# Attention operands of a half loaded in two transfers from relaid scratch, shared weights loaded later, and a new order of the first task's units

## The chip, the cores and the metric

The kernel runs on one core of one Trainium2 chip. Its time is device microseconds of one execution, and the result is compared by the median of several runs. TensorE is PE in the profile, VectorE is DVE, ScalarE is ACT, GpSimd is POOL and SyncE is SP. SP computes nothing here. It issues transfers, and its queue in the profile is SPq.

## The reference, cut to what matters

One transformer layer with modulated layer norms: causal attention with low-rank projections, then a router that sends each token to two of eight experts, and a shared feed-forward branch. Two batches of 1,024 tokens, 128 channels, 16 heads of 8 dimensions.

```python
h = _layernorm(x) * (1 + ca) + sa
Q = ((h @ W_dq) @ W_uq).reshape(B, S, 16, 8)
K = ((h @ W_dkv) @ W_uk).reshape(B, S, 16, 8)
V = ((h @ W_dkv) @ W_uv).reshape(B, S, 16, 8)
attn = softmax(where(causal, Q @ K.T / sqrt(8), -inf))
x = x + ga * (attn @ V) @ W_o
h = _layernorm(x) * (1 + cb) + sb
x = x + gb * (shared_ffn(h) + sum over the 2 chosen experts of w * expert_ffn(h))
```

## The kernel before, in words

**Operands in three parts.** A float32 score is built on PE from bf16 operands. Each of Q and K is split into three bf16 parts, hi, mid and lo. A head has 8 dimensions, so all nine products of parts make a contraction over 3 x 3 x 8 = 72 rows. Lines 840 (hi), 1066 (residue on DVE), 849 (mid) and 613 (lo on POOL) make the parts in the tile `parts`; `QK` numbers the eight pieces (batch, key or query, half of 512 tokens), and the first four (numbers 0 to 3: key and query of half 0, key and query of half 1, batch 0) are made up front, before the unit loop. SP writes the parts to scratch in DRAM (`k_parts`, `q_parts`) and reads them back into the tile `S3`, where each part stands three times, in the pattern that crosses every part of Q with every part of K.

**Tasks.** A task is a batch and a group of four heads, so there are eight, 0 to 7. A task has two halves c of 512 queries. `S3` has three buffers. `load(t)` (three transfers of K by `load_k`, line 477, and three of Q for each half by `load_q`, line 485) waits until the scratch of its batch is written (`parts_out`) and, from task 3 on, until the buffer's last user is done. Task 0 has its own quick path: `store_first` (line 456) and loads of each half alone, counted by `first_in0` and `first_in1`. `store_parts` (lines 463 and 469) writes what the other tasks need.

**Two passes over the scores.** The first pass finds each query's maximum: a `max` unit is up to four matmuls (line 1612) into one of three banks, and a reduction on DVE (line 1231 with the causal mask, line 1235 without). A task has 38 max units, 0 to 10 for half 0 and 11 to 37 for half 1. `maxima` negates them, POOL splits them in three parts (lines 654 to 657), PE turns them (`turn`, line 1621), DVE copies them (line 1252), and SP writes them as three more rows of Q (`neg_rows`, line 502, `negT`). The second pass is 38 `score` units a task (line 1643, with the mask at line 1648), each followed by an exponential on ACT (line 894) and by `weigh`, the products with V (line 1665).

**The order.** `attention_order` writes one list for all engines by hand: 20 max units (`AHEAD`), then for each score unit one score and one max unit, but three max units for each of the first ten scores (`CATCH_UP`). `BETWEEN` puts other work behind named max units: the late turns of x (`xturn`, line 1531), the projections of batch 1 (`proj`, line 1536) and the values (`val`, line 1548). These and the max units share the ring of three banks, save `xturn`. PE takes the list in order, so that a unit that waits holds up all behind it. The matmuls of `fill` (line 1818) compute nothing: two behind each of the first 20 max units, one behind each of the first ten scores.

**SP's order.** SP issues the loads of x and of the small weights, then nine transfers of late weights (line 512: router, `be2`, `bs2`, biases, shared expert; DVE first needs them in `gates_out`, in task 2's max units), then `store_first` and the loads of half 0, the same for half 1, `store_parts(0)`, `neg_rows(0, 0)`, `load(1)`, `neg_rows(0, 1)`, `load(2)`, and from then on `neg_rows` and one load a task.

**After attention** come 39 tiles of routed experts, the gather and the output. The change doesn't touch them.

Of the kernel before, what the change touches and what calls it, by code (L numbers as in the profile page):

```python
# [13 lines left out]
ALU = mybir.AluOpType  # L14
# [3 lines left out]
BF16 = mybir.dt.bfloat16  # L18
# [32 lines left out]
def score_units():  # L51

    out = []
    for c in range(2):
        for j in range(4 * c + 4):
# [19 lines left out]
CATCH_UP = 10  # L75
# [4 lines left out]
BETWEEN = {(0, 7): [("xturn", 2, 0)], (0, 10): [("xturn", 3, 0), ("proj", 4, 0), ("proj", 5, 0)],  # L80
           (0, 14): [("proj", 6, 0)], (0, 18): [("proj", 7, 0)], (0, 23): [("val", 2, 0)], (0, 28): [("val", 3, 0)],
# [26 lines left out]
def attention_order(tasks):  # L108
# [26 lines left out]
    for g in range(tasks * NU):  # L135
# [3 lines left out]
        for _ in range(3 if g < CATCH_UP else 1):  # L139
            next_max()  # L140
# [68 lines left out]
def adaln_layer(nc, x, cT, wmod, wdqT, wdkvT, wuq, wuk, wuv, wo, wr1, br1, wr2, br2,  # L209
# [27 lines left out]
    NLOAD = 9  # L237
# [10 lines left out]
    with ExitStack() as ctx:  # L248
# [3 lines left out]
        def sem(name):  # L252
# [128 lines left out]
        kd = nc.dram_tensor("k_parts", [B, NQ, DK, 3, HQ, S], BF16, kind="Internal").ap()  # L381
        qd = nc.dram_tensor("q_parts", [B, 2, 3, NQ, DK, HQ, HALF], BF16, kind="Internal").ap()
# [11 lines left out]
            var_ready std_ready xn_ready xT_ready hT_ready qk_ready hi_ready r1_ready mid_ready lo_ready  # L394
# [33 lines left out]


        @block.sync  # L430
        def _(sp):
# [17 lines left out]
            def store_first(half):  # L449

                cols = slice(HALF * half, HALF * half + HALF)
                for kq in range(2):
                    for part in range(3):
                        sp.wait_ge((s["hi_ready"], s["mid_ready"], s["lo_ready"])[part], done(0, kq, half))
                        dst = qd[0, half, part, 0] if kq else kd[0, 0, :, part, :, cols]
                        sp.dma_start(dst,
                                     parts[0:HQ * DK, kq, part, cols]).then_inc(s[("k_out", "q_out")[kq]], 16)

            def store_parts(b):
                u0 = 0 if b else 1  # L460
                for part in range(3):
                    sp.wait_ge((s["hi_ready"], s["mid_ready"], s["lo_ready"])[part], done(b, 0, 1))
                    sp.dma_start(kd[b, u0:NQ, :, part, :, :].rearrange("u d h n -> (u d) h n"),
                                 parts[DK * HQ * u0:P, 0, part, b * S:(b + 1) * S]).then_inc(parts_out[b], 16)
                for part in range(3):
                    sp.wait_ge((s["hi_ready"], s["mid_ready"], s["lo_ready"])[part], done(b, 1, 1))
                    for c in range(2):
                        cols = slice(b * S + HALF * c, b * S + HALF * c + HALF)
                        sp.dma_start(qd[b, c, part, u0:NQ, :, :, :].rearrange("u d h n -> (u d h) n"),
# [1440 lines left out]
```

## Time and profile before

| what | value |
|---|---|
| three runs | 446.93, 447.58, 448.43 us; median 447.58 us |
| profiled execution | span 445.2 us from the first to the last instruction, mean granted clock 0.969; its own time is not listed apart from the three runs |
| PE busy | 397.4 us, 89% of the span |
| DVE busy | 326.0 us, 73% |
| ACT busy | 265.9 us, 60% |
| POOL busy | 142.9 us, 32% |
| share of the chain that ended last | PE 69%, DVE 14%, issue 5%, DMA 5% |

The span is 2.4 us below the median of the runs, which also hold what lies before the first and behind the last instruction. Busy shares are averages over stages: the first 25 us set up task 0, 25 to 290 us is attention, 290 to 424 us the experts, and the rest the gather and the output.

### The profile page before, as it was taken

Reading aid. Unit: us, or ns where it says so; the run is one execution under the profiler, and the core shown is the slowest. Engines: PE = TensorE matmul, PEld = TensorE weight load, DVE = VectorE, ACT = ScalarE, POOL = GpSimd, SP = SyncE. Lnnn points to the kernel's source line nnn. Section 1 sums busy time; section 2 is a strip of 40 time slices with the busy share of each in tenths; the row PEclk is TensorE's granted clock in tenths of the full one; section 3 lists DMA queues with packets and bytes.
Section 4 is the critical chain, followed back from the end, with each engine's and each line's share of the span. In section 5 each row is a group of like instructions: output and inputs, shape, how many; then the busy total and the mean of one; then the engine's idle time right before and its main releaser. Section 6 shows DMA issues by size and latency. Waiting matters only on the chain.

```text
span 445.2 us, 9323 instructions
## 1 busy us (share of the span) xinstructions
PE 397.4 (89%) x2901; PEld 231.8 (52%) x2901; DVE 326.0 (73%) x1187; ACT 265.9 (60%) x609; POOL 142.9 (32%) x237
## 2 busy tenths in 40 slices
PE   6679889989999999999989899999989999999900
PEld 3335433443443543545533443434767889999900
DVE  5747799888888887889796887735687665555527
ACT  3623647647666766667665566787756755555632
POOL 2520350000010020105576333504177575334410
PEclk9959999999999999999999999999999999999975
DMA  5433321044040120210210000493012233210153
GB/s 151 144 112 109 94 58 54 1 104 148 1 110 1 35 77 0 67 45 0 68 45 18 21 21 18 116 315 70 7 54 67 73 91 95 68 36 27 37 194 102
DMA packets 28819, 31.77 MB, mean 71 GB/s; under 512 B 4851, under 2 KB 23387, under 8 KB 28267
## 3 DMA queue, kind: packets, MB, share of 16 engines
q1 hardware_dynamic: 26067, 26.12, 21.1%
q0 software_dynamic: 2272, 4.67, 3.1%
q8 instruction: 23, 0.38, 0.4%
q10 hardware_dynamic: 432, 0.39, 0.3%
q14 instruction: 25, 0.20, 0.2%
HBM read 21.04 MB, written 9.85 MB: 69 GB/s over the span
## 4 chain that ended last, share of the span: by engine, by line
PE 69%; DVE 14%; issue 5%; DMA 5%; ACT 3%; POOL 2%; SPq 1%; DVEq 0%; ACTq 0%; POOLq 0%
PE oacc L1665 14%; PE mx L1612 12%; PE sc L1643 11%; PE sc L1798 6%; PE oacc L1811 6%; DVE mxp L1235 3%; DVE masked L1231 3%; PE sc L1648 2%; PE sc L1818 2%; PE mx L1765 2%; PE mx L1674 2%; ACT osb L903 2%; POOL slot_rows L734 2%; PE mx L1754 1%; DMA parts<-token_results 1%
## 5 line engine op out<-in xcount | busy, mean ns | idle before, releaser
L894 ACT ACTIVATE pr<-sc 128x512 f32<-128x512 f32 (+1 forms) x296 | 154.0, 579 | 87.3 <-PE sc L1648 47.6
L1612 PE MATMUL mx<-S 72*128 72x512 bf16 (+3 forms) x384 | 112.8, 331 | 13.6 <-DMA S<-q_parts 6.1
L1231 DVE CUSTOM_DVE_ANT_0 masked<-mx,later 128x128 f32<-128x128 f32 (+3 forms) x256 | 111.6, 485 | 17.0 <-PE mx L1612 16.1
L1643 PE MATMUL sc<-S 75*128 75x512 bf16 (+3 forms) x373 | 108.1, 328 | 0.0
L1235 DVE TENSOR_REDUCE mxp<-mx 128x1 f32<-128x512 f32 x128 | 82.5, 684 | 20.9 <-PE mx L1612 20.5
L1665 PE MATMUL oacc<-pr,vb 128*32 128x512 f32 (+3 forms) x768 | 73.9, 493 | 0.0
L1612 PEld LDWEIGHTS mx<-S 72*128 72x128 bf16 x384 | 34.7, 99 | 52.2 <-DVE mxp L1231 14.8
L958 ACT ACTIVATE pr<-sc,bcur 128x128 f32<-128x128 f32 x156 | 44.6, 369 | 26.6 <-PE sc L1798 26.5
L1643 PEld LDWEIGHTS sc<-S 75*128 75x128 bf16 x373 | 34.5, 97 | 46.4 <-issue 21.2
L740 POOL DMA_INDIRECT token_results<-S,xrow x39 | 39.1, 1003 | 48.0 <-DVE S L1372 44.6
L654 POOL CAST neg<-negm 128x16 bf16<-128x16 f32 x16 | 3.2, 198 | 139.7 <-DVE negm L1244 139.7
L1798 PE MATMUL sc<-xTg,vb 128*128 128x128 f32 x312 | 41.6, 276 | 2.6 <-ACT xTg L950 2.5
L1811 PEld LDWEIGHTS oacc<-vb,pr 128*128 128x128 f32 x312 | 39.0, 192 | 7.2 <-issue 6.0
L1648 PE MATMUL sc<-after,identb 128*128 128x128 bf16 (+2 forms) x172 | 41.9, 244 | 0.0
L1811 PE MATMUL oacc<-vb,pr 128*128 128x128 f32 x312 | 41.3, 275 | 0.3 <-ACT pr L958 0.3
L734 POOL DMA_INDIRECT slot_rows<-parts,rowi x32 | 31.6, 986 | 30.2 <-PE sc L1648 13.6
L1798 PEld LDWEIGHTS sc<-xTg,vb 128*128 128x128 f32 x312 | 37.9, 192 | 3.6 <-ACT xTg L950 3.3
L1665 PEld LDWEIGHTS oacc<-pr,vb 128*32 128x32 f32 x768 | 19.0, 108 | 31.1 <-issue 15.9
L1357 DVE COPY vb<-S 128x512 f32 x39 | 18.4, 472 | 20.8 <-issue 11.3
L1372 DVE TENSOR_TENSOR S<-oacc,be_sb 128x128 f32<-128x128 f32 x39 | 11.3, 290 | 18.0 <-PE oacc L1811 16.4
L1231 DVE DVE_READ_ACCUMULATOR2_ANT mxp<- 128x1 f32 x256 | 21.0, 82 | 0.0
L1648 PEld LDWEIGHTS sc<-after,identb 128*128 128x128 bf16 x172 | 16.8, 98 | 7.4
(279 smaller groups left out, 471.2 us busy)
## 6 DMA issues: line engine op xcount, KB each, us to landing
S<-q_parts SPq DMA_DIRECT2D x48, 96.0 KB
S<-k_parts SPq DMA_DIRECT2D x21, 192.0 KB
xrow<-slot_rows SPq DMA_DIRECT2D x39, 64.5 KB, 1.8
S<-in_we SPq DMA_DIRECT2D x1, 2048.0 KB, 9.1
S<-in_we SPq DMA_DIRECT2D x4, 512.0 KB, 9.9
parts<-token_results SPq DMA_DIRECT2D x4, 512.0 KB, 5.7
x_sb<-in_x SPq DMA_DIRECT2D x4, 256.0 KB, 4.0
out_y<-attn SPq DMA_DIRECT2D x4, 256.0 KB, 2.3
```

What stands on the lines that cost most here:

```text
L734: pool.indirect_dma_start(xd, bass.IndirectOffsetOnAxis(ap=rowi[:, g, k, n:n + 1], axis=0), rowsk[:, g % 2, n, k, :], None).then_inc(sent[ ...
L740: pool.indirect_dma_start(yd, bass.IndirectOffsetOnAxis(ap=xrow[:, i % XR, C:C + 1].bitcast(I32), axis=0), yst[:, i % ROWS, :], None).then ...
L894: act.activation(pr[:, group % NBUF, h:h + n, at:at + w], src, ACT.Exp, scale=float(DK) ** -0.5).then_inc(s["exp_done"], 1)
L958: ins = act.activation(hid[:, i % 2, P * f:P * f + P], sc[:, i % 2, P * f:P * f + P], ACT.Silu, bias=bcur[:, i % FREE, f:f + 1])
L1231: ins = dve.tensor_tensor_reduce(masked[:, d % 2, w * m:w * m + w], unit[a][:, w * m:w * m + w], later[:, HALF - w:HALF], 1.0, LOWEST, ALU ...
L1235: ins = dve.tensor_reduce(mxp[:, c, place, h:h + n, i - 4 * c], unit[a][:, 0:n * w].rearrange("p (h n) -> p h n", h=n), AX_X, ALU.max)
L1612: ins = pe.matmul(dst[:, w * m:w * m + w], S3[0:CROSS, r3, 1, q:q + P], S3[0:CROSS, r3, 0, kk:kk + w], start=(m == 0), stop=True, skip_gro ...
L1643: ins = pe.matmul(dst[:, w * m:w * m + w], S3[0:CROSS + 3, r3, 0, kk:kk + P], S3[0:CROSS + 3, r3, 1, q:q + w], start=(m == 0), stop=True, ...
L1648: ins = pe.matmul(dst[:, 0:n * w].rearrange("p (h n) -> p h n", h=n)[:, :, 0:P], identb[:, :], after[:, 0:n, :], start=False, stop=True, s ...
L1665: ins = pe.matmul(oacc[VW * h:VW * h + VW, c, at:HALF], vb[:, t % 2, j, h, :], pr[:, group % NBUF, h, at:HALF], start=(j == 0), stop=(j == ...
L1798: ins = pe.matmul(sc[:, i % 2, P * f:P * f + P], wcur[:, i % 2, P * f:P * f + P], xTg[:, i % 2, :], start=True, stop=True)
L1811: ins = pe.matmul(oacc[:, i % 2, 0:P], hid[:, i % 2, P * f:P * f + P], wcur[:, i % 2, FF + C * f:FF + C * f + C], start=(f == 0), stop=(f ...
```

## The change

Scratch is laid out anew: `k_parts` by half and part, `q_parts` by half with the parts innermost beside the dimension. The operand rows of a half then load in one transfer for K (72 rows from a source of 24 x 3, each row repeated three times in place) and one for Q (72 rows from a source of 3 x 24, the whole block of 24 rows repeated). A task's load is 4 transfers for 9. The stores are 6 for K and 6 for Q for 3 and 6, and the store of K has an outer extent of three head groups in batch 0 and four in batch 1. The late weights go behind `load(2)`. `store_first` alternates K and Q. `store_parts` becomes `store_keys`, ahead of `neg_rows(0, 0)`, and `store_queries`, behind it. The lo part of piece 1 moves from POOL to DVE, between three and five of the eight statistics of x; ACT takes `hi(2)` ahead of `root(2)`; `residue(3)` goes behind the root's refinement. Fillers are 12 for 50. The first 14 scores are followed by 2 x 9, 4 x 2 and 2 x 3 max units for 3 x 10 and 1 x 4, so that the first max unit of task 1 comes behind score 9 for score 6, and from score 14 on the max units are 38 ahead of the scores for 40.

```diff
-CATCH_UP = 10
+MAXES_AFTER = [2] * 9 + [4] * 2 + [2] * 3
+FILLERS = {(0, k): 2 if k < 3 else 1 for k in (0, 1, 2, 3, 4, 5, 7, 8, 10)}
-BETWEEN = {(0, 7): [("xturn", 2, 0)], (0, 10): [("xturn", 3, 0), ("proj", 4, 0), ("proj", 5, 0)],
-           (0, 14): [("proj", 6, 0)], (0, 18): [("proj", 7, 0)], (0, 23): [("val", 2, 0)], (0, 28): [("val", 3, 0)],
+BETWEEN = {(0, 6): [("xturn", 2, 0)], (0, 9): [("xturn", 3, 0)], (0, 11): [("proj", 4, 0)], (0, 14): [("proj", 5, 0)],
+           (0, 17): [("proj", 6, 0)], (0, 21): [("proj", 7, 0)], (0, 26): [("val", 2, 0)], (0, 31): [("val", 3, 0)],
...
-        for _ in range(3 if g < CATCH_UP else 1):
+        for _ in range(MAXES_AFTER[g] if g < len(MAXES_AFTER) else 1):
...
-        kd = nc.dram_tensor("k_parts", [B, NQ, DK, 3, HQ, S], BF16, kind="Internal").ap()
-        qd = nc.dram_tensor("q_parts", [B, 2, 3, NQ, DK, HQ, HALF], BF16, kind="Internal").ap()
+        kd = nc.dram_tensor("k_parts", [B, 2, NQ, 3, DK, HQ, HALF], BF16, kind="Internal").ap()
+        qd = nc.dram_tensor("q_parts", [B, 2, NQ, DK, 3, HQ, HALF], BF16, kind="Internal").ap()
...
-                for kq in range(2):
-                    for part in range(3):
-                        sp.wait_ge((s["hi_ready"], s["mid_ready"], s["lo_ready"])[part], done(0, kq, half))
-                        dst = qd[0, half, part, 0] if kq else kd[0, 0, :, part, :, cols]
+                for part in range(3):
+                    for kq in range(2):
+                        sp.wait_ge(*part_done(part, QK.index((0, kq, half))))
+                        dst = qd[0, half, 0, :, part] if kq else kd[0, half, 0, part]
...
+            def store_keys(b):
+                u0 = 0 if b else 1
+                for part in range(3):
+                    sp.wait_ge(*part_done(part, QK.index((b, 0, 1))))
+                    for c in range(2):
+                        cols = slice(b * S + HALF * c, b * S + HALF * c + HALF)
+                        sp.dma_start(kd[b, c, u0:NQ, part].rearrange("u d h n -> u (d h) n"),
+                                     parts[DK * HQ * u0:P, 0, part, cols]).then_inc(parts_out[b], 16)
...
-            def load_k(t, cols, sem):
+            def load_k(t, c, sem):
 
                 r3, b, u = place_of(t)
-                src = kd[b, u, :, :, :, cols].rearrange("d a h n -> (d a) h n")
-                for a in range(3):
-                    sp.dma_start(S3[24 * a:24 * a + 24, r3, 0, :].rearrange("r (h n) -> r h n", h=HQ)[:, :, cols],
-                                 src).then_inc(sem, 16)
+                src = kd[b, c, u].rearrange("p d h n -> (p d) (h n)")
+                sp.dma_start(S3[0:CROSS, r3, 0, QW * c:QW * c + QW],
+                             src.unsqueeze(1).broadcast_to([3 * DK, 3, QW])).then_inc(sem, 16)
 
             def load_q(t, c, sem):
 
                 r3, b, u = place_of(t)
-                for a in range(3):
-                    src = qd[b, c, a, u].rearrange("d h n -> d (h n)")
-                    sp.dma_start(S3[24 * a:24 * a + 24, r3, 1, QW * c:QW * c + QW],
-                                 src.unsqueeze(1).broadcast_to([DK, 3, QW])).then_inc(sem, 16)
+                src = qd[b, c, u].rearrange("d a h n -> (d a) (h n)")
+                sp.dma_start(S3[0:CROSS, r3, 1, QW * c:QW * c + QW],
+                             src.unsqueeze(0).broadcast_to([3, 3 * DK, QW])).then_inc(sem, 16)
...
-            sp.wait_ge(x_in[3], 16)
+            for c in range(2):
+                store_first(c)
+                sp.wait_ge(s["k_out"], 48 * c + 48)
+                load_k(0, c, s[f"first_in{c}"])
+                sp.wait_ge(s["q_out"], 48 * c + 48)
+                load_q(0, c, s[f"first_in{c}"])
+            store_keys(0)
+            neg_rows(0, 0)
+            store_queries(0)
+            load(1)
+            neg_rows(0, 1)
+            load(2)
             for dst, src in ((wr1_sb[:, :], wr1), (br1_sb[:, :], br1), (wr2_sb[0:32, :], wr2),
...
-            for n in range(4):
+            for n in (0, 2, 3):
                 low(n, r1[:, n % 2, :])
...
+            hi(2)
             root(2)
-            hi(2)
...
-            aggregate(list(range(8, 16)), s["var_ready"])
+            for n in range(8, 11):
+                tile_stats(n)
+            low(1)
+            aggregate(list(range(8, 16)), s["var_ready"], 3)
             residue(2)
-            residue(3)
...
                                      op0=ALU.mult, op1=ALU.mult).then_inc(s["shift_ready"], 1)
+            residue(3)
...
-                    kk = S * (h0 + m) + k0
+                    kk = key_columns(h0 + m, k0)
...
-                    if t == 0 and k < AHEAD:
-                        fill(sc[:, 2, :], 2)
+                    fill(sc[:, 2, :], FILLERS.get((t, k), 0))
...
-                    if t == 0 and k < CATCH_UP:
-                        fill(oacc[:, 1, :], 1)
```

## Rows read from the trace of the kernel before

**Rows 1.** Busy time by stage (windows), three stages of the span

```profile
core 0: us, PE busy (x) PEld busy (x) DVE busy (x) ACT busy (x) POOL busy (x), PEclk, DMA share, GB/s
20.00:30.00 10.00, 4.65 (x17) 2.34 (x18) 4.23 (x21) 3.59 (x9) 5.21 (x13) 0.57 0.35 101
60.00:70.00 10.00, 9.36 (x69) 3.75 (x66) 9.66 (x40) 4.56 (x9) 5.94 (x10) 1.00 0.41 113
100.00:140.00 40.00, 39.40 (x295) 17.09 (x293) 33.97 (x119) 27.35 (x54) 2.82 (x13) 1.00 0.25 73
```

**Rows 2.** The chain that ended last: start us, us, what; task 0 begins

```profile
25.35 0.59 PE mx L1612 x4
25.93 0.85 PE sc L1818 x2
...
27.21 0.85 PE sc L1818 x2
```

**Rows 3.** SP's queue in order of time: start us, us issuing, line, transfer

```profile
13.15 2.42 SPq L456 DMA_DIRECT2D k_parts<-parts  x3
15.61 1.37 SPq L456 DMA_DIRECT2D q_parts<-parts  x3
18.59 2.40 SPq L477 DMA_DIRECT2D S<-k_parts  x3
21.03 2.05 SPq L485 DMA_DIRECT2D S<-q_parts  x3
...
42.01 0.77 SPq L502 DMA_DIRECT2D S<-negT  x1
```

**Rows 4.** ACT in order of time: last mid part of half 0, normalised x

```profile
14.08 0.63 ACT L849 ACTIVATE parts<-osb 128x512 bf16<-128x512 f32 x1 [0.48 <-DVE osb L1066]
...
21.59 3.18 ACT L875 ACTIVATE attn<-x_sb,shift,rst 128x128 f32<-128x128 f32 x8 [1.18 <-DVE shift L1097]
```

**Rows 5.** DVE in order of time: a residue, and max units of tasks 0 and 1

```profile
13.36 0.68 DVE L1066 TENSOR_TENSOR osb<-oacc,parts 128x512 f32<-128x512 f32 x1
...
42.94 1.88 DVE L1235 TENSOR_REDUCE mxp<-mx 128x1 f32<-128x512 f32 x3
...
58.99 0.29 DVE L1231 CUSTOM_DVE_ANT_0 masked<-mx,later 128x128 f32<-128x128 f32 x1
...
65.96 0.19 DVE L1244 TENSOR_REDUCE negm<-mxp 128x16 f32<-128x32 f32 x1
```

**Rows 6.** PE in order of time: two fillers and the next unit, a weigh

```profile
38.15 0.60 PE L1818 MATMUL sc<-parts,identb 128*128 128x512 bf16 x2
38.58 0.38 PE L1612 MATMUL mx<-S 72*128 72x512 bf16 x1
...
67.50 0.64 PE L1665 MATMUL oacc<-pr,vb 128*32 128x256 f32 x8
```

**Rows 7.** Windows of 1 us: Q loads alone in two tasks, and stores

```profile
48.50:49.50 1.00, 1.00 (x9) 0.85 (x9) 0.87 (x2) 0.02 (x1) 0.00 (x0) 1.00 0.53 193
...
98.50:99.50 1.00, 1.00 (x16) 0.26 (x8) 0.96 (x5) 0.00 (x0) 0.00 (x0) 1.00 0.53 139
...
107.00:108.00 1.00, 1.00 (x9) 0.29 (x12) 1.00 (x6) 0.50 (x2) 0.00 (x0) 1.00 0.84 282
```

**Rows 8.** Window of 0.1 us: the largest share while one `negT` transfer runs

```profile
103.50:103.60 0.10, 0.10 (x3) 0.00 (x0) 0.10 (x1) 0.10 (x1) 0.00 (x0) 1.00 0.25 56
```

**Rows 9.** Windows of 0.5 us: first load's traffic, the clock falls and rises

```profile
19.00:19.50 0.50, 0.20 (x2) 0.01 (x1) 0.50 (x1) 0.50 (x2) 0.50 (x1) 1.00 0.00 0
...
20.00:20.50 0.50, 0.00 (x0) 0.00 (x0) 0.47 (x2) 0.41 (x1) 0.50 (x1) 1.00 0.32 76
...
21.00:21.50 0.50, 0.00 (x0) 0.00 (x0) 0.43 (x3) 0.00 (x0) 0.44 (x2) 0.84 0.55 137
...
31.50:32.00 0.50, 0.50 (x4) 0.31 (x3) 0.10 (x1) 0.00 (x0) 0.00 (x0) 0.92 0.38 131
```

**Rows 10.** DMA issues by line: KB each, median us from issue to landing

```profile
q_parts<-parts SPq DMA_DIRECT2D x6, 32.0 KB, 1.8
```

More of the change, by code:

```diff
@@ L236, in adaln_layer @@
     RING = 3
-    NLOAD = 9
+    NLOAD = 4
     TOK = B * S
@@ L427, in place_of, with low_done, part_done, key_columns @@
             return (t + 1) % 3, t // NQ, t % NQ
+        def low_done(n):
+            return (s["lo1_ready"], 1) if n == 1 else (s["lo_ready"], max(n, 1))
+        def part_done(part, n):
+            return low_done(n) if part == 2 else ((s["hi_ready"], s["mid_ready"])[part], n + 1)
+        def key_columns(h, key):
+            return QW * (key // HALF) + HALF * h + key % HALF
         @block.sync
@@ L451, in store_first @@
                 cols = slice(HALF * half, HALF * half + HALF)
[L452 to L459 removed]
+                for part in range(3):
+                    for kq in range(2):
+                        sp.wait_ge(*part_done(part, QK.index((0, kq, half))))
+                        dst = qd[0, half, 0, :, part] if kq else kd[0, half, 0, part]
+                        sp.dma_start(dst, parts[0:HQ * DK, kq, part, cols]).then_inc(s[("k_out", "q_out")[kq]], 16)
@@ L460, in store_parts @@
+            def store_keys(b):
                 u0 = 0 if b else 1
                 for part in range(3):
[L462 to L466, printed above, removed]
+                    sp.wait_ge(*part_done(part, QK.index((b, 0, 1))))
@@ L512, in _ @@
                 sp.dma_start(dst, src).then_inc(s["w2_in"], 16)
-            for c in range(2):
-                store_first(c)
-                sp.wait_ge(s["k_out"], 48 * c + 48)
-                load_k(0, slice(HALF * c, HALF * c + HALF), s[f"first_in{c}"])
-                sp.wait_ge(s["q_out"], 48 * c + 48)
-                load_q(0, c, s[f"first_in{c}"])
-            store_parts(0)
-            neg_rows(0, 0)
-            load(1)
-            neg_rows(0, 1)
-            load(2)
             for t in range(1, T):
@@ L528, in _ @@
                     if t == 2 and c == 0:
-                        store_parts(1)
+                        store_keys(1)
+                        store_queries(1)
                 if t + 2 < T:
@@ L1043, in rstd, with aggregate @@
                 chained(dve.tensor_tensor(rst[:, ns], rst[:, ns], nwt[:, ns], ALU.mult))
-            def aggregate(ns, done):
+            def aggregate(ns, done, behind=0):
                 ins = None
-                for n in ns:
+                for n in ns[behind:]:
                     ins = dve.bn_stats(stats[:, n, :], x_sb[:, n, :])
@@ L1068, in residue, with low @@
                                   ALU.subtract).then_inc(s["r1_ready"], 1)
+            def low(n):
+                b, kq, half = QK[n]
+                cols = slice(b * S + 512 * half, b * S + 512 * half + 512)
+                dve.wait_ge(s["r1_ready"], n + 1)
+                dve.wait_ge(s["mid_ready"], n + 1)
+                dve.tensor_tensor(parts[:, kq, 2, cols], r1[:, n % 2, :], parts[:, kq, 1, cols],
+                                  ALU.subtract).then_inc(s["lo1_ready"], 1)
             dve.memset(half3[:, :], 1.5)
@@ L1640, in score_unit @@
                 for m in range(n):
-                    kk = S * (h0 + m) + P * j
+                    kk = key_columns(h0 + m, P * j)
                     q = QW * c + HALF * (h0 + m) + q0 - HALF * c
```

22 lines of the change are left out of this document (12 added, 10 removed).

## The prediction, made before the changed kernel was run

> **What bounds the kernel now.** The stages come first [rows 1]. In 20 to 30 us PE is busy 4.65 of 10 us at a granted clock of 0.57; in 60 to 70 us DVE is at 9.66 of 10; from 100 us on PE is at 39.4 of 40. So the setup, then DVE, then PE sets the pace. SP's queue shows the setup [rows 3]: stores from 13.15, loads from 18.59 to 23.08, one after another; PE starts task 0 only at 25.35, when the last Q load has landed [rows 2]. From there the chain runs over PE, max unit and fillers in turn, and through DVE until about 65 us. A microsecond won ahead of 65 us is won at the end, as long as no other wait takes it: behind it PE has the same list to work off.
>
> The last store is issued at 16.98 and the first load waits until 18.59 [rows 3], since the stores queue behind the late weights, which SP issued just before them.
>
> **Part by part: the operands of half 0.** SP is free for the stores when the parts are ready. The last mid part ends at 14.71 [rows 4]. DVE then makes lo of piece 1: its residue of the same size took 0.68 us [rows 5], so it ends at 15.4, beside lo of piece 0 on POOL, which made both in turn before; DVE's statistics fill its wait. Stores cost SP 0.46 us each where the scratch is contiguous and 0.8 where it is not [rows 3]; K now is contiguous, so K lo goes out at 15.4 and Q lo from 15.9. Without the weights ahead I take 1.8 us to land [rows 10]. K is there at 17.2 and Q at 17.8. A load costs 0.68 us of issue [rows 3], two in all where six took 4.5 us. SP issues Q at 17.8.
>
> **What the one Q transfer costs** is the term that decides. Before, the source of a Q load had an outer extent of eight rows, and while only such loads run, the DMA share is 0.53 of 16 engines, so eight of them work [rows 7]. A `negT` transfer has three outer rows, and its share is never over 0.25, so no more than four [rows 8]. The new Q load has an outer extent of three (the block of 24 rows, three times). I take three engines. An engine moved 193/(16 x 0.53) = 22.8 GB/s in the first window and 139/(16 x 0.53) = 16.4 in the second [rows 7]. A half's Q is 72 x 4 KB = 0.295 MB, so 4.3 us at the first rate and 6.0 us at the second; on eight engines it would be 1.6. I take the first rate, since nothing else runs here. With 1.5 us from issue to first bytes (K was issued at 18.59 and its traffic stands in the window from 20.0, [rows 3, 9]) and 0.6 us to the signal, which I estimate, PE starts at 17.8 + 1.5 + 4.3 + 0.6 = 24.2, only 1.15 us earlier than 25.35 [rows 2].
>
> The trace thus puts about as many engines on a transfer as its outer extent. The Trainium skill ("DMA: Bandwidth & Descriptors", section on why a DMA increments its semaphore by 16) states it as a rule: the number of engines is the largest up to 16 that divides the slowest dimension of both sides. By it K's load (24 and 72) gets 12, Q's three, and the key stores of batch 0 (three head groups) three. The sum would be the same, and it speaks against this layout.
>
> **The first 38 max units.** On DVE the eleven units of a half 0 take 58.99 to 65.96 = 7.0 us, the same masked shapes stand in half 1, and its 16 plain units are 0.63 each [rows 5]: 24.0 us in all. Before, from PE's first to DVE's first of task 1, they took 25.35 to 58.99 = 33.6 us [rows 2, 5], for PE had fillers between: 0.43 a pair at the full clock [rows 6], 0.85 at half [rows 2]. The order has 12 fillers for 50. What is left over the 24.0: the clock fell at 21.3, 1.9 us behind PE's last work at 19.4, and rose at 31.5, 6.2 us behind its restart [rows 9]; PE stays idle 4.8 us in the new kernel, so it starts at 1.2 GHz again. Three units with two fillers then pace at 1.28 us (25.93 to 27.21, [rows 2]) against some 0.8 on DVE, and three with one at 0.75 against 0.5: 2.2 us. The six late projections and values take a bank of the ring; I charge 0.4 us each, half the 0.86 us that four float32 passes of 512 columns take at the rate of the fillers [rows 6]: 2.4 us. DVE would be done at 24.2 + 0.7 + 24.0 + 2.2 + 2.4 = 53.5. The turn of x waits for nothing: its inputs come from 21.59 us on [rows 4], and it stands behind unit 6, after 28 us. The 0.7 is DVE behind PE.
>
> **What is late next.** The stores of keys go in six transfers of 96 KB on three engines, by the reasoning above: 0.197 MB an engine at 282/(16 x 0.84) = 21.0 GB/s [rows 7] is 9.4 us. They queue behind the Q load of half 1, which ends at about 31, so they occupy these engines until 40.4. `neg_rows(0, 0)` is also on three, behind them: it lands at 41.2, where score 0 would be due at about 39.5. PE waits 1 to 2 us, which the next wait swallows. SP issues six query stores from about 36 to 40.5, they land at 42.9, and `load(1)` begins to move at 44.4. On the busiest engines it is K 2 x 25 KB plus Q 2 x 98 KB = 0.246 MB: 10.8 us at 22.8 GB/s, 15.0 at 16.4. It lands at 55.7. Max unit 0 of task 1 waits for it, and all of PE's list behind it, so PE resumes task 1 at 55.7 and DVE at 56.1, against 58.99 before: 2.9 us won, not the 5.5 that DVE's sum would allow.
>
> **Behind it.** Then DVE sets the pace as before for eleven units. Before, DVE ended them at 65.96; now at 63.1. The order has scores 11 and 12 and a weigh already done at this point (0.22 each, half of a pair of fillers, and 0.6, [rows 6]): 1.0 more. Two max units are deferred to the end: 0.4 back. `neg_rows(0, 1)` now has four units between the turn and its score; issue 0.77 [rows 3] and 1.5 to land make a wait of about 0.8, of which DVE's queue hides half: 0.3 back. Sum: 2.9 + 1.0 - 0.4 - 0.3 = **3.2 us**.
>
> At nothing I cost: the late weights behind `load(2)` (first used in task 2's max units at some 95 us, moved by about 75); later loads, 10 to 15 us on three engines for 8 to 10 on eight, but due about 20 us after they are issued; the 12 stores of batch 1 (7 us of SP, with some 15 us to the next `neg_rows`); `key_columns`, the same matmuls. If that cover were gone, each task could lose up to 5 us. `hi(2)` ahead of `root(2)` and `residue(3)` behind the refinement move half 1's operands by 0.5 us, with 2 us to spare.
>
> The median is 447.58 and the profiled span 445.2; I expect 442.0 of span and **444.4 us**.
>
> **The rivals.**
>
> A. The Q load is not held to three engines. For it: a transfer of 12 KB in 0.1 us windows is thin evidence for one of 295 KB. Then Q lands by 17.8 + 1.5 + 1.6 + 0.6 = 21.5, DVE is done with task 0's units at 50.8, `load(1)` is there before, and the gain is 58.99 - 50.8 + 0.3 = 8.5 us: 439.1. Chance 0.14.
>
> B. The clock. With few fillers PE does little between the units, and the granted clock, 0.5 from 21.5 to 31.5 [rows 9], stays low until about 40. Then PE paces units and projections at twice their time for 8 us more, 3 us lost: 447.2, no change. Against it: in 60 to 70 us PE held 1.00 at 9.4 of 10 busy, but these rows don't show the clock with PE at half its time. Chance 0.12.
>
> C. Slower. Place: `load(1)`. If three engines move at 16.4 GB/s, as eight did at 98.5 us [rows 7], the Q of half 0 lands 1.7 us later, key stores (12.0 us for 9.4) end at 43 to 44.5, and the load takes 15.0: it lands near 61.5. Then task 1 begins 5.8 us later than I forecast, 2.6 us over before: 450.2. It decides from a landing past 58.9 us, and past 60.3 us the kernel is slower by over 0.3%. The trace shows both rates for the same kind of transfer. Chance 0.13.
>
> **How the numbers follow.** The forecast has 0.61: the sum of terms with a load at 19 to 23 GB/s, 442 to 446.5. The bounds of single terms give about 441.5 (load at 25 GB/s, key stores hidden) to 447. Range 440.3 to 448.9: it leaves out most of A and half of C. A measurement here tells about 0.3%, 1.35 us, from no change. Faster by more: forecast 0.60, A 0.14 and a little of B, 0.75. Within: most of B, the slow edge of the forecast, the near side of C, 0.13. Slower: C, 0.12.
>
> **What would show each step.** The Q load of half 0: DMA share about 0.19 for 4 us ahead of PE's first max unit at 24.2 (A: share 0.5 or more and a start near 21.5). Clock: up by 28 to 32 us; if still 0.5 at 36, B. Max unit 0 of task 1: PE idle in front of it, released by the DMA of S, at 55 to 56 us; if it is released by DVE, the load was no bound and I am too slow by some 3 us; if it stands past 59 us, C. Score 0: a wait of 1 to 2 us on `negT`. Behind 66 us the distance to the old trace should stay within 1 us; were it to shrink in each task, the loads of later tasks are late, and I am wrong in what I cost at nothing.

## The result, and the profile after

The change makes the kernel **slower by 0.8%**: 452.95 us median of 8 runs (450.1 to 453.8) against 448.77 (446.93 to 450.26) for the kernel before, run beside it, ratio 1.0079 [1.005, 1.0107]. I had forecast 444.4, in a range of 440.3 to 448.9. The profiled execution took 450.1 us with a span of 448.4, 3.2 more than before; it is the quickest of the eight.

Lines move in the new file: max units stand at 1639, scores at 1670, the turn at 1648, the fillers at 1845, `load_k` at 493, `load_q` at 500, the key stores at 477, the query stores at 486, `neg_rows` at 517.

The page of the changed kernel, busy time by engine and the chain that ended last by engine:

```profile
PE 399.4 (89%) x2863; PEld 226.7 (51%) x2863; DVE 322.5 (72%) x1188; ACT 266.3 (59%) x609; POOL 141.3 (32%) x236
...
PE 70%; DVE 11%; DMA 8%; issue 4%; POOL 2%; SPq 2%; ACT 1%; DVEq 0%; POOLq 0%; ACTq 0%
```

PE is busy 2 us longer although it has 38 fillers fewer, and DMA has gone from 5% to 8% of the chain. What PE waited for between 20 and 300 us (engine, line, releaser, us in total, times, longest):

```profile
PE mx L1639 <- DMA S<-q_parts: 10.5, 3, 7.2
PE mx L1639 <- DVE mxp L1258: 2.3, 4, 0.7
PE sc L1670 <- DMA S<-negT: 2.0, 1, 2.0
```

Before, the operands were waited for once, 6.15 us; now three times, and `negT` once. In PE's order of time these four waits are (start us, us, ..., [idle before, releaser]):

```profile
27.18 0.58 PE L1639 MATMUL mx<-S 72*128 72x128 bf16 x4 [7.20 <-DMA S<-q_parts]
...
36.33 0.38 PE L1639 MATMUL mx<-S 72*128 72x512 bf16 x1 [1.42 <-DMA S<-q_parts]
...
44.93 0.58 PE L1670 MATMUL sc<-S 75*128 75x512 bf16 x1 [2.03 <-DMA S<-negT]
...
60.78 0.82 PE L1639 MATMUL mx<-S 72*128 72x128 bf16 x8 [1.91 <-DMA S<-q_parts]
```

Task 0 starts at 27.18 for 25.35 [rows 2]. The second row is unit 11, the first of half 1; the third is score 0; the last is the first max unit of task 1. Its operands land 13.4 us after SP began to issue `load(1)`, as SP's queue shows (start us, us issuing, line, transfer; the rows of [rows 3]):

```profile
16.22 0.44 SPq L469 DMA_DIRECT2D k_parts<-parts  x1
16.70 0.63 SPq L469 DMA_DIRECT2D q_parts<-parts  x1
18.92 0.80 SPq L493 DMA_DIRECT2D S<-k_parts  x1
19.76 0.74 SPq L500 DMA_DIRECT2D S<-q_parts  x1
...
28.76 0.73 SPq L500 DMA_DIRECT2D S<-q_parts  x1
29.54 8.27 SPq L477 DMA_DIRECT2D k_parts<-parts  x6
40.20 0.72 SPq L517 DMA_DIRECT2D S<-negT  x1
40.97 4.74 SPq L486 DMA_DIRECT2D q_parts<-parts  x6
47.33 0.78 SPq L493 DMA_DIRECT2D S<-k_parts  x1
```

Windows of the changed kernel (columns as in [rows 1]): the Q load of half 0, the Q loads of `load(1)`, the gap before task 1, what follows, and ten microseconds of the experts for later.

```profile
24.00:27.00 3.00, 0.00 (x0) 0.00 (x0) 0.00 (x0) 2.23 (x6) 2.56 (x8) 0.54 0.21 77
...
53.00:59.00 6.00, 5.75 (x37) 2.68 (x37) 4.83 (x13) 4.57 (x11) 4.16 (x4) 1.00 0.20 77
...
57.00:62.00 5.00, 2.66 (x20) 1.32 (x18) 3.51 (x16) 2.60 (x6) 4.62 (x6) 0.98 0.11 44
62.00:79.00 17.00, 16.80 (x68) 5.03 (x68) 11.97 (x45) 5.16 (x9) 1.76 (x8) 0.50 0.45 128
...
340.00:350.00 10.00, 10.00 (x66) 7.68 (x66) 7.29 (x28) 6.12 (x19) 7.31 (x8) 1.00 0.27 67
```

and of the kernel before, the same two last stretches:

```profile
57.00:62.00 5.00, 4.21 (x27) 1.54 (x28) 4.96 (x27) 3.05 (x6) 2.58 (x7) 1.00 0.02 5
62.00:79.00 17.00, 16.62 (x112) 6.24 (x111) 15.39 (x50) 10.42 (x20) 4.02 (x7) 1.00 0.26 72
```

Two things stand out. The share is 0.20 to 0.21 while Q loads alone: about three engines of 16 (3/16 is 0.19), at 77/(16 x 0.21) = 23 to 77/(16 x 0.20) = 24 GB/s each. And PE, busy 2.66 of 5 us before 62 us where it had 4.21, goes through the next 17 us at 1.2 GHz: 68 matmuls where the kernel before had 112 in the same time at 2.4 GHz. I had not priced that. It is not the only stretch: behind the wait for `negT` the clock was at 0.50 too. It fell in the first of these two windows and rose in the second.

```profile
44.50:45.00 0.50, 0.07 (x1) 0.10 (x2) 0.00 (x0) 0.00 (x0) 0.00 (x0) 0.73 0.45 135
...
48.00:48.50 0.50, 0.50 (x4) 0.28 (x3) 0.00 (x0) 0.29 (x1) 0.00 (x0) 0.86 0.00 0
```

Where the loss stands later is seen at the turns of attention's output, 60 matmuls from task 0 to task 7 (duration in ns, first and last start, shape), first before, then after:

```profile
L1674 PE MATMUL mx<-ident,osb x60: 272/273/328, 70.8 to 294.1; 128*128 128x128 f32 x60
```

```profile
L1701 PE MATMUL mx<-ident,osb x60: 272/273/421, 75.4 to 297.4; 128*128 128x128 f32 x60
```

4.6 us late at the first, 3.3 at the last: it is made ahead of the first and doesn't grow. Of the 4.6, 2.2 us are there when DVE begins task 1 (before: 58.99, [rows 5]); the other 2.4 come behind it, while PE is at 1.2 GHz. DVE's first row of task 1:

```profile
61.20 0.29 DVE L1258 CUSTOM_DVE_ANT_0 masked<-mx,later 128x128 f32<-128x128 f32 x1 [1.06 <-PE mx L1639]
```

### The profile page after: what moved, and what is told of

The parts are those of the page before. It is cut to its first block, busy times and chain, and to the rows that moved or that the text cites. A ratio compares the mean times of both kernels' runs of the same rounds, so it can differ in the third digit from the quotient of the medians.

```text
span 448.4 us, 9210 instructions
## 1 busy us (share of the span) xinstructions
PE 399.4 (89%) x2863; PEld 226.7 (51%) x2863; DVE 322.5 (72%) x1188; ACT 266.3 (59%) x609; POOL 141.3 (32%) x236
## 4 chain that ended last, share of the span: by engine, by line
PE 70%; DVE 11%; DMA 8%; issue 4%; POOL 2%; SPq 2%; ACT 1%; DVEq 0%; POOLq 0%; ACTq 0%
PE oacc L1692 14%; PE mx L1639 14%; PE sc L1670 13%; PE sc L1825 6%; PE oacc L1838 6%; DMA S<-q_parts 4%; PE sc L1675 3%; PE mx L1792 2%; PE mx L1701 2%; POOL slot_rows L749 2%; PE mx L1781 1%; DVE mxp L1262 1%; DMA k_parts<-parts 1%; DVE masked L1258 1%; DVE parts L1522 1%
## 5 line engine op out<-in xcount | busy, mean ns | idle before, releaser
L1639 PE MATMUL mx<-S 72*128 72x512 bf16 (+3 forms) x384 | 115.1, 342 | 15.9 <-DMA S<-q_parts 10.5
L1670 PE MATMUL sc<-S 75*128 75x512 bf16 (+3 forms) x374 | 111.0, 334 | 2.0 <-DMA S<-negT 2.0
L1262 DVE TENSOR_REDUCE mxp<-mx 128x1 f32<-128x512 f32 x128 | 81.4, 684 | 24.3 <-PE mx L1639 24.0
L1692 PE MATMUL oacc<-pr,vb 128*32 128x512 f32 (+3 forms) x768 | 76.1, 505 | 0.0
L1670 PEld LDWEIGHTS sc<-S 75*128 75x128 bf16 x374 | 35.6, 99 | 50.0 <-issue 25.9
L1692 PEld LDWEIGHTS oacc<-pr,vb 128*32 128x32 f32 x768 | 19.2, 110 | 35.4 <-issue 20.8
```

The source lines that it names most:

```text
L1262: ins = dve.tensor_reduce(mxp[:, c, place, h:h + n, i - 4 * c], unit[a][:, 0:n * w].rearrange("p (h n) -> p h n", h=n), AX_X, ALU.max)
L1639: ins = pe.matmul(dst[:, w * m:w * m + w], S3[0:CROSS, r3, 1, q:q + P], S3[0:CROSS, r3, 0, kk:kk + w], start=(m == 0), stop=True, skip_gro ...
L1670: ins = pe.matmul(dst[:, w * m:w * m + w], S3[0:CROSS + 3, r3, 0, kk:kk + P], S3[0:CROSS + 3, r3, 1, q:q + w], start=(m == 0), stop=True, ...
L1692: ins = pe.matmul(oacc[VW * h:VW * h + VW, c, at:HALF], vb[:, t % 2, j, h, :], pr[:, group % NBUF, h, at:HALF], start=(j == 0), stop=(j == ...
```

## The experiments

There were two theories. **Loads**: the transfers on three engines cost the start and each wait behind it, and that alone makes the kernel slow. **Clock**: the order with few fillers leaves PE thin at the turn from task 0 to task 1, and the clock falls there whatever the loads do. The twelve runs came in three groups of four; ratios are to the kernel before, run beside each group. That stood at 448.18 us (446.38 to 449.86, 25 runs) in the first group, 448.53 (447.13 to 454.93, 13 runs) in the second and 462.54 (460.13 to 470.01, 25 runs) in the third, so times of the third compare only by ratio. The record numbers the chip of the first group 13 and that of the second and the third 11, so nothing on record puts the third group's longer times down to another chip. "Low" is the mean granted clock in 57 to 62 and in 62 to 79 us, from windows as those above.

| run | us | ratio [95%] | low | waits of PE for `q_parts` |
|---|---|---|---|---|
| changed (three engines for Q) | 452.95 | 1.0079 [1.005, 1.0107] | 0.98, 0.50 | 10.5 us, 3 times |
| `e1_spread` | 445.83 | 0.9943 [0.9921, 0.9964] | 0.50, 0.55 | 5.1, 2 |
| `e2_qsplit` | 445.41 | 0.995 [0.9928, 0.9972] | 0.53, 0.74 | 4.3, 1 |
| `e3_fillers` | 454.86 | 1.0154 [1.0105, 1.0204] | 1.00, 0.53 | 10.9, 2 |
| `e6_weights_order` | 446.19 | 0.9945 [0.9917, 0.9974] | 0.56, 0.53 | 5.1, 1 |
| `e4_weights` | 446.84 | 0.9977 [0.9953, 1.0001] | 1.00, 1.00 | 4.8, 1 |
| `e7_keep` | 443.04 | 0.9844 [0.977, 0.9918] | 0.89, 1.00 | 5.4, 2 |
| `e8_pool` | 443.42 | 0.9888 [0.9837, 0.994] | 0.60, 0.72 | 4.5, 1 |
| `e9_both` | 438.64 | 0.9771 [0.9728, 0.9814] | 1.00, 1.00 | 4.9, 1 |
| `a0_changed` (third group) | 466.33 | 1.0048 [1.0008, 1.0089] | 0.98, 0.50 | 11.1, 3 |
| `e5_order` (third group) | 460.14 | 0.9937 [0.9901, 0.9972] | 0.55, 0.63 | 5.4, 1 |
| `e10_after_both` (third group) | 462.84 | 0.9992 [0.9942, 1.0041] | 1.00, 1.00 | 8.4, 3 |
| `e11_old_loads_both` (third group) | 453.3 | 0.9765 [0.9683, 0.9848] | 1.00, 1.00 | 5.3, 1 |

### The three engines

`e2_qsplit` takes the changed kernel and writes each Q load as three transfers of 24 rows; the counts that `first_in` and `load` wait for follow. `e1_spread` also splits the key stores by head group.

```diff
-                sp.dma_start(S3[0:CROSS, r3, 1, QW * c:QW * c + QW],
-                             src.unsqueeze(0).broadcast_to([3, 3 * DK, QW])).then_inc(sem, 16)
+                for x3 in range(3):
+                    sp.dma_start(S3[24 * x3:24 * x3 + 24, r3, 1, QW * c:QW * c + QW], src).then_inc(sem, 16)
```

> The changed kernel with only the Q loads in three transfers; the key stores stay on three engines. Theory 1: start near 24 us, task 1 not late, but score 0 still waits 1 to 3 us for negT behind the key stores; the clock may dip once near 45 us; 441 to 446 us. Rival 2: as with the other spread kernel, 446 to 450.

In `e1_spread` besides:

```diff
+                        for u in range(u0, NQ):
+                            sp.dma_start(kd[b, c, u, part].rearrange("d h n -> (d h) n"),
+                                         parts[DK * HQ * u:DK * HQ * u + DK * HQ, 0, part, cols]).then_inc(parts_out[b], 16)
```

> The changed kernel, with only the transfers spread over more engines: a half's Q in three transfers of 24 rows (12 engines each) and the key stores in one transfer per head group (32 rows, 16 engines). Theory 1 (the three-engine transfers make the waits, and the waits make the clock fall): PE starts task 0 near 24 us for 27.2, no waits of PE for S at units 11 (1.4 us), score 0 (2.0 us) or task 1 (1.9 us), the clock stays up from about 31 us on, and the time is 439 to 443 us, 0.98 to 0.99 of the kernel before. Rival 2 (too few fillers let the clock fall whatever the loads do): waits gone, but the granted clock is 0.5 again somewhere between 35 and 80 us for 10 us or more, and the time is 446 to 450 us.

Splitting Q alone gives 445.41, ratio 0.995 where the change stood at 1.0079: the loss is gone and a gain of 0.5% is there. SP's queue and windows of `e2_qsplit`:

```profile
18.72 0.80 SPq L493 DMA_DIRECT2D S<-k_parts  x1
19.56 1.35 SPq L501 DMA_DIRECT2D S<-q_parts  x3
...
27.34 4.89 SPq L477 DMA_DIRECT2D k_parts<-parts  x6
36.96 0.72 SPq L517 DMA_DIRECT2D S<-negT  x1
37.72 4.74 SPq L486 DMA_DIRECT2D q_parts<-parts  x6
44.06 0.78 SPq L493 DMA_DIRECT2D S<-k_parts  x1
```

```profile
21.50:22.50 1.00, 0.00 (x0) 0.00 (x0) 0.00 (x0) 1.00 (x3) 0.28 (x1) 1.00 0.88 238
...
52.00:57.00 5.00, 2.60 (x20) 1.29 (x21) 4.77 (x26) 1.98 (x4) 4.41 (x8) 1.00 0.02 6
57.00:62.00 5.00, 4.72 (x18) 1.09 (x16) 3.40 (x12) 0.95 (x2) 0.00 (x0) 0.53 0.40 98
62.00:79.00 17.00, 17.00 (x90) 5.84 (x88) 12.85 (x41) 9.12 (x18) 0.83 (x4) 0.74 0.48 111
```

While Q loads beside the end of K the share is 0.88, no stretch at 0.21 follows ahead of task 0, and PE starts at 24.21, 3.0 us sooner. The waits for half 1, for `negT` and for `load(1)`, which is issued 3.3 us sooner, don't appear in it; I had expected the one for `negT` to stay, since the key stores are still on three engines. The six key stores take SP 4.89 us where they took 8.27. Splitting them as well (18 transfers, 8.23 us of SP) gives 445.83 for 445.41: nothing. So of the two transfers that I put on three engines, the Q load carried the loss. (Both times, and that of `e6_weights_order` below, are medians over executions of two kinds: of the ten of `e2_qsplit` the two quickest, 443.69 and 444.5 us, have a mean clock of 0.955 and 0.956, the others, 445.2 to 446.7, of 0.944 to 0.949. The profile is of the quickest.)

But both runs have a new stretch at 1.2 GHz, from 57 us on, though no load is late in `e2_qsplit` (and `load(1)` by only 0.8 us in `e1_spread`). At that place PE and then POOL have these rows:

```profile
56.57 0.24 PE L1648 MATMUL mx<-identb,neg 128*48 128x128 bf16 x1 [1.16 <-POOL neg L672]
```

```profile
50.55 2.39 POOL L628 TENSOR_TENSOR parts<-attn,parts 128x512 bf16<-128x512 f32 x2 [1.76 <-ACT parts L864]
53.02 2.38 POOL L628 TENSOR_TENSOR parts<-hT,parts 128x512 bf16<-128x512 f32 x2
55.47 0.20 POOL L669 CAST neg<-negm 128x16 bf16<-128x16 f32 x1
```

In 52 to 57 us DVE is at 4.77 of 5 and PE at 2.60: the first units of task 1, masked, each short for PE and long for DVE, and then the turn of task 0's second maxima, for which PE waits 1.16 us until POOL, busy with the low parts of batch 1, has split them. Behind it the clock is down with PE fully busy.

### The order and the fillers

`e3_fillers` is the changed kernel with the 50 fillers of before (two behind each of the first 20 max units, one behind each of the first ten scores).

```diff
-FILLERS = {(0, k): 2 if k < 3 else 1 for k in (0, 1, 2, 3, 4, 5, 7, 8, 10)}
+FILLERS = {(0, k): 2 for k in range(20)}
...
+                    if t == 0 and k < 10:
+                        fill(oacc[:, 1, :], 1)
```

> The changed kernel with the 50 fillers of before (two behind each of the first 20 max units, one behind each of the first ten scores), transfers on three engines. Theory 1: the start stays at 27 us and the waits for the load of task 1 at 58 to 61 us stay, so the clock still falls near 62 us; 451 to 455 us. Rival 2: the clock stays up from 34 us on, and the time falls below that of the changed kernel by 3 us or more, to 446 to 449.

454.86, so with the loads as they are the fillers that were removed would not have helped. In its trace `load(1)` is what task 1 waits for, longer than before, and the clock is at 0.53 in the 17 us behind it:

```profile
63.06 1.44 PE L1639 MATMUL mx<-S 72*128 72x128 bf16 x8 [3.61 <-DMA S<-q_parts]
```

The clock is at 1.00 in 44 to 54 us, where the changed kernel had 0.83: these fillers keep the clock in task 0, and the fall in task 1 stays.

`e4_weights` is the kernel before with only the late weights behind `load(2)`; `e6_weights_order` adds the new order and its 12 fillers; `e5_order` has the order without the weights. The edit of the order, cut:

```diff
-CATCH_UP = 10
+MAXES_AFTER = [2] * 9 + [4] * 2 + [2] * 3
+FILLERS = {(0, k): 2 if k < 3 else 1 for k in (0, 1, 2, 3, 4, 5, 7, 8, 10)}
```

> The kernel before with nothing but the late weights moved behind the second load: old layout, old order, 50 fillers. Theory (the weights held up the first stores by about 1 to 2 us): PE starts task 0 near 24 us for 25.3, the clock keeps the pattern of before, 445.5 to 447.5 us, a ratio of 0.996. Rival (they cost nothing, the setup waits for the parts): same as before within 0.2%.

> The kernel before with the late weights behind the second load, the new order and the 12 fillers, but the old scratch layout and the old three-transfer loads. Theory 1: PE starts at 23 to 24 us, task 1's load is there in time, the clock stays up, 441 to 444 us, 0.985 to 0.99 of before. Rival 2: the clock falls as in the changed kernel, 446 to 450 us.

> The kernel before with the new order of the first task's units and the twelve fillers alone: old layout, old loads, weights where they were. Theory (the order wins a little time by itself and pays some of it back in a clock that falls at the turn to task 1): the kernel with order and late weights stood at 446.2 and the one with the late weights alone at 446.8, against 448.5 of before, so the order should give 446 to 448 with the clock at 0.5 for over 12 us after 55 us, and the first unit should wait about 5 us for its operands. Rival (the order by itself costs time, and only the earlier start of the late weights pays for it): over 449.

The weights alone 0.9977 (its interval touches 1), the order alone 0.9937, both 0.9945. By these three ratios the order gives more than the weights, and the two hardly add (added up they would give 0.991; the intervals are too wide to be sure). With the order the clock falls after 57 us (0.56 and 0.53), with the weights alone it stays at 1.00. The 460.14 us of `e5_order` lie outside the 446 to 448 expected, as all times of the third group do. And `e6_weights_order` (old layout, nine transfers a task) is level with `e2_qsplit` (new layout, Q split): 0.9945 and 0.995.

### What keeps the clock

`e7_keep` puts two fillers behind each of task 1's first eleven max units of `e2_qsplit`. `e8_pool` moves the low parts of batch 1 four groups later in the same kernel, so that POOL splits the maxima first. `e9_both` does both.

```diff
+KEPT = {(1, k): 2 for k in range(11)}
...
-HI_AT, RES_AT, MID_AT, LOW_AT = 2, 3, 6, 7
+HI_AT, RES_AT, MID_AT, LOW_AT = 2, 3, 6, 11
...
                     fill(sc[:, 2, :], FILLERS.get((t, k), 0))
+                    fill(oacc[:, 1, :], KEPT.get((t, k), 0))
```

> The changed kernel with Q split in three transfers, and two more fillers behind each of the first eleven max units of task 1. Theory 3 (what is left of the loss is the clock, which falls near 57 us because PE is thinly busy from 52 to 57 us, where DVE and a wait for POOL set the pace): the granted clock stays at 1.0 through 50 to 80 us, and the time is 438 to 441.5 us, 4 us below the same kernel without them (445.4). Rival (the fall comes from PE's wait for POOL at the turn alone, which fillers cannot cover): the clock still falls near 57 us, and the time is 445 to 447 us.

> The changed kernel with Q split in three transfers, and POOL's four lo parts of batch 1 put off by four score units, behind the split of the maxima of half 1 of task 0. Theory 3: PE's wait of 1.2 us for POOL at the turn is gone, PE is a little busier there, and the clock falls in part of the executions only; 440 to 445 us. Rival: the lo parts are no part of it, and time and clock stay as without the edit, 445 to 446.

> Both edits, the fillers in task 1's first units and POOL's lo parts later, on the changed kernel with Q split. Theory 3: the clock stays up, 437.5 to 441 us, the fastest of all. Rival: 444 to 446, the clock falls all the same.

Against `e2_qsplit` (ratio 0.995) they stand at 0.9844, 0.9888 and 0.9771. `e7_keep` missed the 438 to 441.5 us that I had expected; of its four executions one, with the highest mean clock (0.971), took 438.67 us, and the others, at 0.959 to 0.963, 442.6 to 444.0. In the profile, of a slower one, PE waits 1.26 us for `load(1)` at 54.4 us, and the clock falls behind that wait in spite of the fillers. Each alone leaves a stretch at 1.2 GHz in its profile: in `e7_keep` the clock is 0.77 in 52 to 57 us, in `e8_pool` 0.60 and 0.72 behind 57. With both it stays up, in windows of `e9_both`:

```profile
52.00:57.00 5.00, 4.46 (x31) 2.32 (x30) 4.96 (x28) 2.02 (x5) 2.33 (x7) 1.00 0.04 10
57.00:62.00 5.00, 5.00 (x29) 2.00 (x28) 3.78 (x14) 0.93 (x2) 3.43 (x3) 1.00 0.31 94
62.00:79.00 17.00, 17.00 (x117) 6.26 (x118) 14.78 (x47) 11.81 (x23) 0.83 (x4) 1.00 0.43 114
```

22 matmuls that compute nothing and one step of POOL moved by four groups are worth 445.41 - 438.64 = 6.8 us between medians of two groups, and 1.8% by the ratios. How much of it is the clock alone is not separated: moving the step also takes away PE's wait of 1.16 us. PE does 117 matmuls in 62 to 79 us where `e2_qsplit` did 90 and the changed kernel 68. DVE is busy in 52 to 57 for 4.96 us against 4.77, so the fillers took nothing from the engine that sets the pace there.

### The third group

`a0_changed` is the changed kernel again; `e10_after_both` is it with the two edits of `e9_both` and the Q loads left on three engines; `e11_old_loads_both` is `e6_weights_order` with the two edits.

> The changed kernel once more, as the measure for the other three on one chip. It should stand at 450 to 454 us, 0.5 to 1.3% above the kernel before, with the granted clock at 0.5 for some 14 to 20 us between 57 and 80 us. If it stood below the kernel before here, the first result was the chip's and not the change's, and every conclusion drawn from differences across chips would have to be looked at again.

> The changed kernel with its Q loads left on three engines, but with two fillers behind each of task 1's first eleven maximum units and the low parts of batch 1 made eleven groups into the task. Theory (two separate losses: 7 us at the start through the three-engine loads, and about 7 us through the half clock after 57 us): the clock should stay at 1.0 past 57 us, and the time should be the changed kernel's less 5 to 8 us, 444 to 447, while the first unit still starts past 27 us and the wait for Q stays at 9 to 11 us. Rival (the clock falls because the loads come late, so fillers can't keep it without the split): the clock is at 0.5 for over 10 us after 55 us all the same, and the time is 450 or more.

> The kernel before with the late weights, the new order, and the same two edits (fillers in task 1's first eleven units, low parts later), on the old layout and the old loads. It shows what the relaid scratch is worth once it is loaded over enough engines: the same kernel on the relaid scratch with Q in three transfers stood at 438.6. Theory (the relaid scratch with split Q wins nothing beyond the few tenths by which its first operands land earlier; the same pair without these two edits stood at 445.4 and 446.2): 438.5 to 440.5. Rival (the layout wins by itself, since six fewer issues ahead of each half bring the second half's operands sooner): 441 to 444.

The changed kernel is slower again, by less: 1.0048 [1.0008, 1.0089]. Its 466.33 us lie outside the 450 to 454 expected, since every kernel took longer in this group, that of before included. In the trace of `a0_changed` the extra time stands behind attention, in code that the change doesn't touch. The last turn of attention's output starts at 298.3 us, 0.9 later than in the first profile, but the span is 465.4 for 448.4, 17.0 longer. Among the experts, engines wait for releasers outside the core's own engines ("remote"; engine, line, releaser, us, times, longest), which the first profile doesn't have:

```profile
ACT pr L973 <- remote: 11.6, 2, 7.6
```

No trace shows the kernel before in this group. The turns of `a0_changed` and of `e10_after_both`:

```profile
L1701 PE MATMUL mx<-ident,osb x60: 272/273/421, 76.1 to 298.3; 128*128 128x128 f32 x60
```

```profile
L1702 PE MATMUL mx<-ident,osb x60: 272/273/332, 73.1 to 294.1; 128*128 128x128 f32 x60
```

`e10_after_both` wins 3.5 us on `a0_changed` by the medians and 4.2 us by the start of the last turn, below the 5 to 8 of the theory. Windows of `e10_after_both`:

```profile
44.00:54.00 10.00, 9.67 (x32) 5.34 (x33) 5.17 (x16) 5.78 (x11) 3.20 (x3) 0.50 0.40 115
...
62.00:79.00 17.00, 17.00 (x109) 6.52 (x108) 14.82 (x56) 7.73 (x15) 6.12 (x11) 1.00 0.50 129
```

and of `a0_changed`:

```profile
44.00:54.00 10.00, 8.20 (x37) 4.00 (x37) 6.24 (x22) 6.63 (x13) 3.54 (x4) 0.83 0.42 121
...
62.00:79.00 17.00, 16.72 (x71) 5.15 (x69) 12.64 (x51) 5.16 (x9) 1.72 (x8) 0.50 0.45 125
...
340.00:350.00 10.00, 7.08 (x28) 4.91 (x26) 4.60 (x12) 5.75 (x18) 5.99 (x7) 0.57 0.22 60
```

The fall after 57 us is gone, but this doesn't separate the theory from its rival. The fall around 44 us, behind the wait for `negT`, was 10 us long in this execution and held PE back, so that PE reached task 1 late and hardly waited for `load(1)`, 0.23 us where `a0_changed` waited 2.63:

```profile
60.29 0.38 PE L1640 MATMUL mx<-S 72*128 72x128 bf16 x4 [0.23 <-DMA S<-q_parts]
```

So the late loads keep a fall of their own; whether the two edits would hold the clock behind a long wait for `load(1)` is not shown, and the two losses don't add up: with both edits three engines for Q cost 0.9992 - 0.9771 = 2.2%, without them 1.0079 - 0.995 = 1.3%. `e11_old_loads_both` is at 0.9765 [0.9683, 0.9848] where `e9_both` was at 0.9771: with both edits, too, the relaid scratch is worth nothing that these runs can tell. (Its 453.3 us lie outside the expected 438.5 to 440.5 as all times of this group do; the ratio to before is the one that the theory gave.)

**The best version** that ran is `e9_both`: 438.64 us (437.76 to 439.47), 2.3% below the kernel before; `e11_old_loads_both` is as good by ratio and keeps the old layout.

## Why the prediction was wrong

**The Q load on three engines: right.** Share 0.20 to 0.21, as the outer extent of three said, and the rival with more engines (A) is refuted. By the count of engines that the Trainium skill gives ("DMA: Bandwidth & Descriptors", why a DMA increments its semaphore by 16), which I cited, the trace agrees. The rate was 23 to 24 GB/s an engine where I took 22.8.

**The start: 24.2 forecast, 27.18 measured.** Two of the 3.0 us lie ahead of the load. ACT's last mid part ended at 15.50, not at the 14.71 of [rows 4], so SP issued Q mid at 15.52 and, taking K and Q in turn, K lo behind it at 16.22 for 15.4 and Q lo at 16.70 for 15.9. Low of piece 1 on DVE (0.89 us from 15.60) was done by then. K lo then needed 2.7 us until SP could go on (16.22 to 18.92) where I took the 1.8 of [rows 10]. Q was issued at 19.76 for 17.8. The remaining microsecond is 7.4 from issue to start for my 1.5 + 4.3 + 0.6. I had written that nothing else runs here, but SP issued the six stores of half 1 from 20.55 on, and the share is above that of the Q load alone until 24 us; how much they took from its three engines isn't shown. The start was meant to be 1.15 us ahead of before and was 1.8 behind. ACT's last mid part, and a window with the stores:

```profile
14.87 0.63 ACT L864 ACTIVATE parts<-osb 128x512 bf16<-128x512 f32 x1 [0.24 <-DVE osb L1081]
```

```profile
23.50:24.00 0.50, 0.00 (x0) 0.00 (x0) 0.00 (x0) 0.50 (x3) 0.46 (x1) 1.00 0.49 133
```

**DVE's 38 units: right in the sum.** I had 24.0 + 2.2 + 2.4 = 28.6 us. In the trace they run from 27.92 to 59.92, 32.0 us, with 1.4 for half 1 and 2.0 for `negT`; without these 28.6. Its parts fit less well: DVE waited 0.23, 0.50 and 0.25 us for PE ahead of units 1, 2 and 3, 1.0 in all where I had 2.2 for the low clock, and so some 3.6 are left where I had 2.4 for projections and values. That the sum fits is in part luck.

**The step that failed first: the way to `load(1)`.** The chain was right, its terms were too small. The wait for `negT` was forecast at 1 to 2 us and is 2.03. The wait of 1.42 us for half 1's operands I had not seen: SP issued that Q load at 28.76, behind the Q load of half 0 and the six stores. So `negT` goes at 40.20, the query stores end at 45.71 (40.5 forecast), and `load(1)` lands at 60.8, 5.1 us past my 55.7: 4.4 of it there when the load was issued (3.0 of the start, 1.4 of the half), 0.7 the transfer. DVE begins task 1 at 61.20, against 58.99 before. I had 2.9 us won here; it is 2.2 lost, 5.1 of the 6.4 us by which the span missed (448.4 for 442.0). The place of rival C was right (60.8 is past its 60.3), but its cause, a rate of 16.4 GB/s, was not; the time was lost before the load was issued.

**The step that had no price: the clock.** I wrote "clock up by 28 to 32 us" and gave no price to anything behind. Rival B looked for a low clock in the wrong place, in task 0 until 40 us, at 3 us; there it rose by about 31 us. It fell from about 44.7 to 48.1 us and again, for 17 us, in task 1. At the first turn of attention's output the kernel is 4.6 us behind where I had it 3.2 ahead: 5.1 of these 7.8 us are the late start of task 1, and 2.7 stand behind it. (1.3 us come back until the last turn; why is not shown.) That DVE sets the pace there [rows 1] I had read, and the 9.36 of 10 us busy at 1.00 as comfort. But those ten microseconds hold scores, fillers and a weigh among the units: before, a score and a filler stood ahead of every three of task 1's first units. The new order has a score ahead of every four of the first eight and no filler, and I credited the work done earlier with 1.0 us without asking what PE would do in its place. In `e2_qsplit`, where `load(1)` is in time, PE is 2.60 of 5 us busy and then at 1.2 GHz; the two edits that undo it, the removed wait for POOL among them, are worth 6.8 us. In [rows 9] PE's last work ahead of the restart ends at 19.2, not at the 19.4 that I read; the sum doesn't change by it.

**At nothing I cost** later loads, query stores of batch 1 and late weights. Behind task 1 no wait for a DMA is among PE's waits, so this holds. The low parts of batch 1 on POOL were not in my list at all: before, task 0's maxima were complete behind score 5 and their split stood ahead of these parts, which go with group 7; now they are complete behind score 8, and the split stands behind the parts, 1.2 us of PE in `e2_qsplit`.

**The account.** The two failed steps in ratios: with Q split and the clock still falling the kernel is at 0.995, with the loads as they are and the two edits for the clock at 0.9992, with both at 0.9771. By ratios: order and weights -0.5%; relaid scratch with Q split: nothing (0.995 against 0.9945); Q on three engines +1.3%. Sum +0.8%. (With the 1.0048 of `a0_changed` for 1.0079 the three engines cost 1.0%.) I forecast a gain of 0.7%. The order and the weights give 0.5% when Q isn't held to three engines, and with the two edits that keep the clock up 2.3%.

**Open.** Why the six key stores take SP 8.27 us in one kernel and 4.89 in the other; and how the loss of 1.3% by the three-engine load divides between the waits and the falls of the clock near 44 and 62 us. `e10_after_both` puts the second fall at 3.5 us, with medians of 10 runs whose ranges overlap, a longer first fall in its profile and hardly a wait for `load(1)`, so that is no bound. Whether the fall at 62 us of the changed kernel came from the 1.91 us of waiting there, from the thin work or from both is open with it; `e2_qsplit` shows only that the thin work and the wait for POOL suffice. Why the last mid part came 0.8 us later is open too.

## What to carry to other kernels

Fewer transfers need not be faster ones: look at the outer extent of both sides before merging, and read the DMA share while one of them runs. When an order takes independent matmuls away from a stretch that another engine paces, ask how busy PE is left there and what its clock does behind it; fillers belong in that stretch, not only at the start. And a step that is due "just in time" (POOL's split of the maxima) is put ahead of bulk work on the same engine.

## What the runs showed of the hardware

The clock stayed low with PE fully busy for 17 us. In the changed kernel PE was busy 16.80 of 17 us at 0.50; in `e6_weights_order` 17.00 of 17 at 0.53. It fell after stretches in which PE was partly busy (2.60 of 5 us in `e2_qsplit`), not idle. In `e2_qsplit` the longest idle time in that stretch was 1.16 us; in `e9_both`, with PE busy 4.46 of the same 5 us, the clock stayed at 1.00. The Trainium skill ("TensorE: Matmul & The Clock Gate", Part 1) says of the ramp at the start of PE's work that for modelling it costs under 1% of a typical kernel's span. What was avoided here is a later fall, which that sentence doesn't speak of: the two edits against it gave 6.8 of 445.4 us, 1.5%, with the removed wait of 1.16 us in it.

The time behind attention differs between groups of runs of the same kernel. In 340 to 350 us, among the experts, `a0_changed` was at 0.57 with PE busy 7.08 of 10 us, where the first profile of the same kernel had 1.00 and 10.00 (last row of each kernel's windows above). Its median is 466.33 for 452.95, and its engines wait there for something remote, up to 7.6 us at a time on ACT. What that is, is open.
